# Attention, routing and shared expert on one Trainium2 core: the hand-over written out, the last pair's routing chain re-cut, the routing steps of all pairs placed anew

## The reference

```python
x = x + layernorm(attention(layernorm(x)))      # 16 heads of 128, mxfp4 weights and scales, biases
x = x + layernorm(ffn(layernorm(x)))

def ffn(x):                                     # 4096 tokens
    scores = softmax(x @ gate_weight.T)         # 64 experts in 8 groups of 8
    # the 3 best groups by their best score; in them the 6 best experts: topk_w, topk_i
    pos = rank of this token within its expert  # in order of tokens
    slot = expert * 96 + minimum(pos, 95)       # capacity 96: later tokens overwrite row 95
    buf[slot] = x[token]
    out = (silu(buf @ Wg.T) * (buf @ Wu.T)) @ Wd.T   # per expert, 176 hidden
    y = sum over the 6 picks of out[slot] * topk_w
    shared = (silu(x @ Sg.T) * (x @ Su.T)) @ Sd.T    # every token, 352 hidden
    return y + shared
```

## Time and profile before

| | |
|---|---|
| median of 3 runs (lowest, highest) | 1286.58 us (1281.99, 1288.19) |
| the profiled execution | 1283.75 us, of which the span of the trace is 1282.0 us |
| TensorE busy | 1184.0 us, 92% of the span |
| VectorE, ScalarE, GpSimd busy | 903.6, 867.0, 667.9 us |
| mean granted TensorE clock | 0.983 |
| share of TensorE, of DMA, of "issue" in the chain that ended last | 62%, 10%, 9% |

### The profile page before, as it was taken

The page is one execution under the profiler, slowest core; times in us unless marked ns, Lnnn a source line. Parts: engine busy times, 40 slices in busy tenths (PEclk is TensorE's granted clock), DMA queues, the critical chain, the costliest instruction groups (busy, mean ns, idle before and its releaser), DMA issues.

```text
span 1282.0 us, 25190 instructions
## 1 busy us (share of the span) xinstructions
PE 1184.0 (92%) x7600; PEld 837.4 (65%) x7600; DVE 903.6 (70%) x2657; ACT 867.0 (68%) x2320; POOL 667.9 (52%) x746
## 2 busy tenths in 40 slices
PE   4899999999999999999999999999868899999995
PEld 1566676766667666666666666676534577777973
DVE  3787688799889889979988987887765222222336
ACT  3998779878878877887887787788544322323413
POOL 4564334235655665555656556556454524444557
PEclk9999999999999999999999999999979999999997
DMA  7687577767876566574555456455446278898676
GB/s 269 156 215 141 113 131 150 176 145 165 195 181 137 115 128 104 97 125 98 94 113 102 93 108 125 78 96 114 74 114 198 80 213 242 221 247 221 132 211 209
DMA packets 394758, 190.01 MB, mean 148 GB/s; under 512 B 317520, under 2 KB 373302, under 8 KB 394624
## 3 DMA queue, kind: packets, MB, share of 16 engines
q1 hardware_dynamic: 375040, 173.53, 59.0%
q0 software_dynamic: 16416, 11.70, 5.1%
q10 hardware_dynamic: 3168, 3.15, 0.7%
HBM read 75.32 MB, written 64.69 MB: 109 GB/s over the span
## 4 chain that ended last, share of the span: by engine, by line
PE 62%; DMA 10%; issue 9%; POOL 7%; DVE 5%; ACT 4%; SPq 1%; another core or an unknown queue 1%; POOLq 0%; ACTq 0%; DVEq 0%
PE bank L1079 14%; PE bank L1108 13%; PE bank L1123 10%; DMA Y<-W,wix 8%; PE bank L1094 7%; PE bank L1140 7%; PE bank L1172 3%; POOL BUF L757 3%; PE bank L1248 2%; PE bank L1261 2%; POOL P L1009 1%; PE bank L1207 1%; POOL PH L1014 1%; DMA X<-in_x 1%
## 5 line engine op out<-in xcount | busy, mean ns | idle before, releaser
L1350 ACT ACTIVATE P<-bank,nm 128x256 f32<-128x256 f32 x512 | 237.8, 471 | 95.5 <-DVE nm L1519 93.5
L1079 PE MATMUL bank<-RB,W 128*128 128x512 f16 x1076 | 275.8, 382 | 1.4 <-DVE RB L471 1.4
L1108 PE MATMUL bank<-RB 128*128 128x256 f32 x1024 | 245.5, 383 | 11.2 <-issue 7.1
L757 POOL DMA_INDIRECT BUF<-RT,ix x192 | 197.3, 1028 | 84.7 <-issue 44.5
L1009 POOL TENSOR_SCALAR P<-P,rr 128x256 f32<-128x256 f32 x256 | 124.5, 497 | 208.4 <-DVE rr L1501 204.5
L1108 PEld LDWEIGHTS bank<-RB 128*128 128x128 f32 x1024 | 185.5, 191 | 38.5 <-issue 8.6
L1079 PEld LDWEIGHTS bank<-RB,W 128*128 128x128 f16 x1076 | 105.8, 98 | 118.6 <-issue 3.0
L1519 DVE TENSOR_REDUCE nm<-bank 128x2 f32<-128x512 f32 x256 | 174.3, 681 | 6.1 <-PE bank L1108 5.7
L1014 POOL TENSOR_TENSOR PH<-P,PH 128x512 f16<-128x512 f32 x86 | 104.0, 1209 | 111.4 <-ACT PH L1366 111.1
L1140 PE MATMUL bank<-W,O 128*128 128x256 f16 x1060 | 157.8, 273 | 1.6 <-DVE O L1525 1.6
L1030 POOL DMA_INDIRECT Y<-W,wix x64 | 90.8, 1419 | 116.4 <-ACT W L1430 77.3
(11 more groups left out here) (223 smaller groups left out, 1991.0 us busy)
## 6 DMA issues: line engine op xcount, KB each, us to landing
RB<-in_ewT SPq DMA_DIRECT2D x24, 352.0 KB
BUF<-zrow SPq DMA_DIRECT2D x24, 321.0 KB, 3.4
W<-BUF SPq DMA_DIRECT2D x64, 120.4 KB
HT<-in_ewT SPq DMA_DIRECT2D x18, 352.0 KB
HT<-in_wc SPq DMA_DIRECT2D x24, 256.0 KB, 4.5
HT<-in_ws SPq DMA_DIRECT2D x24, 256.0 KB, 5.1
Y<-zrow SPq DMA_DIRECT2D x20, 256.0 KB
RB<-in_ewd SPq DMA_DIRECT2D x24, 176.0 KB
```

Source lines behind the costliest of these rows:

```text
L757: eng.indirect_dma_start(BUF, bass.IndirectOffsetOnAxis(ap=ix[:, rt, t, k:k + 1], axis=0), RT[:, rt, t, :], None, bounds_check=CAP * E - 1 ...
L1079: r = eng.matmul(bk_[:, :], W[:, m, a, c * 2048 + h * 128:c * 2048 + (h + 1) * 128], XT[:, bp % 2, b, c, :], start=(k == 0), stop=(k == n ...
L1108: r = eng.matmul(bS[u % 2][:, t * 256:(t + 1) * 256], QK[:, i % 2, 0, q * 256 + t * 128:q * 256 + (t + 1) * 128], QK[:, i % 2, 1, q * 256: ...
L1350: r = eng.activation(P[:, u % 2, t * 256:(t + 1) * 256], bS[u % 2][:, t * 256:(t + 1) * 256], ACT.Exp, bias=nm0[:, u % 4, t:t + 1], accum_ ...
```

## The change

Four things change.

1. **The drain slots 253 to 259 get lists of their own** (`DRAIN`). `U1` leaves slot 258 and becomes the first piece of the tail. `WO` in slots 256 to 259 is bundled behind `PV`. The conversion of the shared expert's weights (`hi_w`, `lo_w`) has named places, ScalarE's `O` stands ahead of its last `P`, and the first silu `s0` and product `a0` stand in slots 255 and 256, within attention, where before they stood behind 17 chain steps of the last pair.
2. **The tail has a new order.** TensorE does `U1` to `U4` and `D0` at once; the chain is threaded through later pieces.
3. **The last pair's chain is shorter or split.** Its two normalizations are shared between VectorE and ScalarE (two tiles each), its two transposes go to separate PSUM banks, the division by the softmax sum moves from ahead of the group choice to the six weights and behind the ranks' input `M`, the mask of kept ranks (`KP`) goes (ranks from 95 on are now dropped by the DMA's bound), the indices come before the `W95` weights, the counts `Ms`, `MC` are left out for the last pair, and `last_tokens` stands among the last 24 scatters, ahead of the 15th, not behind the 24th. All pairs get the shortened routing; `pos` waits for `M` alone.
4. **`PLACE`, `W_AT`, `CHECK_AT`, `TURN_X`, `TURN_P`, `STORE_AT`, `KEEP_AT`, `SHARED_AT` and the `ORDER` of odd slots have new numbers.** In steady state the order of the large operations on TensorE stays the same.

```diff
 ORDER = {'pe': ([('S', 0), ('S', -1), ('Q', -2), ('V', -6), ('K', -2), ('PV', 4), ('WO', 6), ('bg', 0)],
-        [('PV', 4), ('WO', 6), ('bg', 0)]),
+        [('PV', 4), ('bg', 0), ('WO', 6)]),
...
- 'pool': ([('bg', 0)], [('bg', 0), ('norm', 0), ('lo', 0), ('bg', 0), ('bg', 0)]),
+ 'pool': ([('bg', 0)], [('norm', 0), ('bg', 0), ('lo', 0), ('bg', 0)]),
...
-               (32, 0), (32, 3), (32, 4), (32, 4), (33, 1), (33, 4), (33, 4), (34, 0), (34, 2), (34, 4),
+               (30, 5), (31, 0), (31, 3), (32, 2), (32, 4), (33, 3), (33, 3), (33, 6), (34, 1), (34, 2),
...
-TAIL_ORDER = {'pe': 'U2 U3 c34 U4 c37 U5 c40 D0 U6 U7 c60 U8 U9 D1 U10 U11 U12 D2 U13 U14 U15 D3 c74 U16 U17 D4 D5 c84',
- 'dve': 'c17 a0 c19 l0 c22 a1 c32 l1 a2 c36 a3 c39 l2 l3 c43 a4 c54 a5 c57 l4 c59 a6 l5 c61 a7 c62 l6 c64 l7 '
+TAIL_ORDER = {'pe': 'U1 U2 U3 U4 D0 U5 U6 U7 c39 U8 c44 U9 D1 U10 c64 U11 D2 U12 U13 U14 c73 U15 D3 U16 U17 D4 D5',
+ 'dve': 'c6 l0 c7 a1 c10 a2 c12 l1 c15 a3 c17 l2 c20 a4 c26 l3 c29 a5 c36 l4 l5 a6 a7 c43 l6 c47 l7 '
...
+STEPS = ("U", "D", "s", "h", "a", "l", "hi_w", "lo_w")
+DRAIN = {
+    ("pe", 256): [("U", 0), ("PV", 4), ("bg", 0)],
+    ("pe", 257): [("PV", 4), ("WO", 7), ("WO", 6), ("bg", 0)],
+    ("pe", 258): [("PV", 4), ("bg", 0)],
+    ("pe", 259): [("PV", 4), ("WO", 7), ("WO", 6), ("bg", 0)],
+    ("act", 253): ORDER["act"][1] + [("hi_w", 0), ("hi_w", 1)],
+    ("act", 255): [("bg", 0), ("P", 1), ("bg", 0), ("O", 5), ("P", 0), ("s", 0), ("hi_w", 2), ("bg", 0)],
...
+    ("dve", 256): [("bg", 0), ("O", 6), ("bg", 0), ("a", 0), ("bg", 0), ("lo_w", 2), ("bg", 0)],
...
-REST = {(6, 11): 2, (6, 18): 5, (7, 3): 10, (7, 6): 11, (7, 9): 12, (7, 12): 13, (7, 15): 14, (7, 18): 15, (7, 21): 16}
+REST = {(6, 11): 2, (6, 18): 5, (7, 3): 11, (7, 6): 12, (7, 9): 13, (7, 12): 14, (7, 15): 15, (7, 18): 16, (7, 21): 17}
+LB_AT = 14
...
+            if at is whole:
+                n = ch.n
...
+                yield ch.step("dve", at("dve"), two, waits)
+                yield ch.step("act", at("act"), others, [(ch.sem, n)] + list(waits), alone=True)
...
-            PO.step("dve", at("dve"), lambda e: e.reciprocal(grec[:, :], gsum[:, :]))
-            PO.step("dve", at("dve"), lambda e: e.tensor_tensor(Sx[:, :, :], Sx[:, :, :],
-                                                              grec[:, :].unsqueeze(2).broadcast_to([128, 4, E]), ALU.mult))
...
-            PO.step("dve", at("dve"), lambda e: e.scalar_tensor_tensor(
-                out=KP[:, :, :], in0=pp, scalar=CAP - 1.5, in1=M[:, :, :], op0=ALU.is_lt, op1=ALU.mult))
...
-        plan["pool"].setdefault(END + 101, []).append(last_tokens)
+        plan["pool"][END + 100].insert(LB_AT, last_tokens)
```

More of the change, by code:

```diff
@@ L88, in slot_work @@
 def slot_work(who, u, work):
-    order, part = ORDER[who][u % 2], 0
+    order, part = DRAIN.get((who, u), ORDER[who][u % 2]), 0
     for j, (name, lag) in enumerate(order):
@@ L94, in slot_work @@
             work["at"](u, j)
-        if name in FIRST:
+        if name in STEPS:
+            work[name](lag)
+        elif name in FIRST:
             assert w % 2 == 0
@@ L191, in step, with place @@
         return self.n
+    def place(self, engine, fn):
+        self.plan[engine].setdefault(self.tail + self.tails, []).append(fn)
+        self.tails += 1
 def build(nc, x, wc, wsc, wo_c, wo_s, bqkv, bo, gateT, sguT, sdT, ewT, ewd, out):
@@ L426, in four, with two, others @@
                 return r
-            if at is whole or at is first:
+            if at is whole:
+                n = ch.n
+                def two(eng):
+                    for t in range(2, 4):
+                        r = eng.tensor_scalar(dst(t), src(t), NW[which][:, 1, t:t + 1], NW[which][:, 3, t:t + 1],
+                                              ALU.mult, ALU.add)
+                    return r
+                def others(eng):
+                    for t in range(2):
+                        r = one(t)(eng)
+                    return r
+                yield ch.step("dve", at("dve"), two, waits)
+                yield ch.step("act", at("act"), others, [(ch.sem, n)] + list(waits), alone=True)
+            elif at is first:
                 yield ch.step("act", at("act"), four, waits)
```

139 lines of the change are left out of this document (83 added, 56 removed), and 14 rows, old and new, of tables (ORDER, PLACE).

## The result

The changed kernel takes 1276.04 us (median of 20 runs, 1271.57 to 1281.47), the kernel before beside it 1282.88 us (20 runs). The ratio is 0.9954, 95% interval 0.9942 to 0.9966: 6 us faster, clear of noise, and within the 0.5% that I called no change. I had forecast 1268 from a median of 1286.6, a gain of 18.5. The profiled execution took 1277.07 us, its span is 1275.3.

The account below looks back on a forecast made before the run. TensorE was taken to bound steady attention, GpSimd's path the new tail. 1283.75 - 3.8 (end of attention) - 16.7 (tail) + 2 (steady attention) = 1265.3 us profiled; median 2.8 above, 1268; range 1255 to 1281.

Parts of the forecast that it names:

- the tail: From attention's end to the first expert: 78 us against 94.7, a gain of 16.7 us, bounds 71 and 87 us.
- My sum for TensorE: TensorE's work in the tail: 17 pieces U, 6 pieces D, 2.2 us for the rest, plus small allowances: 73 us.
- rival 3: Something else sets the first experts: two stalls like ScalarE's 9.18 us, or transfers, lose 15 us: 1283 us; chance 0.13.
- GpSimd's path: In the tail, indices, 24 scatters and gather, landing and read take longer than TensorE: 75.5 us, with stretched scatters 78.
- the indices: Last pair's indices in the tail, ready 38.6 us after attention's end instead of 44.3.
- End of attention: Drain from `U0` to attention's last matmul: ends 3.8 us earlier, 0.8 from `O`, 3.1 from `U1` leaving; bounds 1 and 5.
- Steady attention: Seven pairs: +4.5 us from a new wait, 2.5 credited for shorter chains, +2 taken in all; bounds -14 and +14.
- `W95`'s wait: In slot 34, the next K projection waits 0.6 to 0.7 us for the rank bank's last reader, seven times: +4.5 us.
- rival 2: New places close the gaps at slot 12 and ahead of `pos`: 13.7 us gained instead of +2, 1252 us; chance 0.13.
- rival 4: Slower: the wait for `W95` shifts `exp` and K's copy, slot after slot; 4 us a pair gives 1294 us; chance 0.07.
- Row 95 hidden: In the tail, gather and write of row 95, 2.92 + 3.26 us, lie beside the last ten scatters.
- rival 1: Scatters are stretched: all 25 take 0.48 us more, 12 us less the 2.5 allowed, 1277.5 us; chance 0.17.

Follow-up runs that it names:

- plain DMAs: Changed kernel with the 48 last scatters replaced by plain DMAs of the same bytes from GpSimd's queue to a scratch tensor: 1255.28 us, ratio to the kernel before 0.9768.
- W95 first: Changed kernel with the W95 weights of pairs 0 to 6 taken ahead of the top eight: 1257.12 us, then 1273.77; ratios to the kernel before 0.991 and 0.9895.

## Why the prediction was wrong

**The step that failed** is the tail, "against 94.7 the tail gains 16.7 us": it gained 1.6 us in the first pair of traces and 5.6 when quiet. The forecast had 78 us; the runs have 93.1 (late) and 81.6 (quiet). Taken apart, 16.7 is 5.6 that came when quiet, 7.5 that the baseline held too much, and 3.6 by which GpSimd's path was longer than forecast; in the late condition 4.0 of the 5.6 are lost again.

- *Its baseline.* 7.5 of the 94.7 us belong to the late condition (87.20 when quiet). I took the one event that I saw, 9.18 us in the earlier trace rows, for a rival with a chance of 0.13 and left it in the baseline; yet ScalarE waited there for a TensorE that had been done for 4.3 us, beside scatters.
- *Its mechanism.* My sum for TensorE, 73 us, is right when nothing is late: 73.2 to 74.5 us without the scatters. The new tail runs `U`s and `D`s with little slack beside the same 48 scatters, so a late completion that is needed stops TensorE, and most stops are followed by slow clock. From the quiet tail to the late one that is 11.5 us. I had no term for it; rival 3 comes nearest (two such stalls, 15 us, 1283), with a chance of 0.13. The kernel before loses as much (1267.5 to 1282.9 us between the conditions; the changed one 1263.1 to 1276.0), so the ratio hardly shows it.
- *GpSimd's path*, which I took for the end, is the end when quiet. 81.60 = 44.13 to the first scatter + 32.83 for the 24 scatters and the gather + 4.64 for landing and read. I had 39.4 + 32.0 + 4.1 + 2.5. The mis-sized term is the indices: ready at +43.4, forecast +38.6. VectorE stood still with norm steps queued behind `a1`, `a2` and `a3`:

```profile
935.64 0.69 DVE L1605 SCALAR_TENSOR_TENSOR W<-bank,W 128x512 f32<-128x512 f32 x1 [3.69 <-ACT W L1448]
938.63 0.69 DVE L1605 SCALAR_TENSOR_TENSOR W<-bank,W 96x512 f32<-96x512 f32 x1 [1.84 <-ACT W L1448]
941.23 0.69 DVE L1605 SCALAR_TENSOR_TENSOR W<-bank,W 128x512 f32<-128x512 f32 x1 [0.57 <-ACT W L1448]
970.53 0.18 DVE L809 TENSOR_SCALAR ix<-c 128x32 uint32<-128x32 f32 x1
```

That is 6.1 us of waiting where I had charged only the 3.5 us that the products themselves take. It is argued and not shown that this made the indices late: with the norms ahead of these products they came at +43.7, no earlier, since other steps then held the chain.

**End of attention** (-3.8): -0.7 when quiet, +2.4 in the first traces. `PV` came at 3.5 us after `U0`, near my 3.2, and the next `PV` waits 2.27 us for `O`, where I had 2.6. What I had not charged in this stretch is slow clock behind that wait: the eight `WO` ran at a granted clock of 0.50 (1.91 us against 1.05) in these traces, and of the late one's 19.50 us another 3.5 are the late `O` (a wait of 5.17 where 1.63 stands when quiet). Without the scatters in the late condition, and with plain DMAs, the same 2.27 us were followed by full clock (1.04 us), and the stretch was 13.5 us; I had 13.3. So the order of the pieces can give what I forecast; why the clock falls behind one such wait and not behind another is open. With W95 first the stretch was 13.7 us in three kernels of four.

**Steady attention** (+2): `W95`'s wait is 0.65 us, as forecast, but six times and not seven, and W95 first shows that it costs 3.3 to 4.4 us in all. What I credited against it gives a net of -0.5 when quiet. The wait ahead of `pos`, which I kept, went: V's projection has one now (0.76 us). The gap at slot 12 stayed (0.8 to 1.4 us), which speaks against rival 2, and `U0` did not come later, against rival 4. The sum was off by 2.5 us; the 6.9 us of the first traces did not come from the change alone.

**Right:** the experts unchanged; `a0` and `U1` without the last pair. Row 95 hidden beside the scatters fits the quiet trace (the rows come 4.6 us after the last scatter's issue ends, without gather or write between), though the run that put the gather last could not test it. **The scatters themselves** were not stretched (rival 1): of the changed kernel's last 48 the median took 0.97 us and the longest 1.56. The Trainium skill ("SBUF — State Buffer", section "SBUF: two separate sides") says that VectorE in its two-port mode keeps GpSimd from writing the descriptors of its DMAs, and it made me look for slower scatters. These rows don't show that; they show scatters that delay the news of TensorE's work.

## What to carry to other kernels

A trace holds the kernel and the condition in which it ran: an engine that stands still on a "remote" releaser, when its producer had ended long before, is a mark of the condition, and has to be taken out of the baseline before a gain is counted against it. It pays to profile the kernel before twice, in two sessions. Where indirect DMAs run one behind another, it may help to leave slack between TensorE's pieces and their readers, or to keep the scatters away from the stretch where every piece waits for the one before; neither was tried here. And a wait that can be named in a trace (here W95, six times 0.65 us) was worth more than the new tables, which gave nothing when quiet.
